# Start of an attention and expert kernel: constants awaited by user, contexts and zero rows by early DMAs, x's statistics in smaller parts

## The chip, the cores and the metric

The kernel runs on one core of a Trainium2 chip. The metric is the device time of one execution in microseconds, as the median of several runs. One profiled execution gives the trace that is read here.

## The reference

x is 32 batches of 100 rows of 256, ctx is 32 batches of 361 rows. All in fp32:

```python
def xattn(encoded, decoded, ...):             # 16 heads of 16
    q = decoded @ Wq.T + bq; k = encoded @ Wk.T + bk; v = encoded @ Wv.T + bv
    attn = softmax(einsum('bhqd,bhkd->bhqk', q, k)); z = einsum('bhqk,bhkd->bhqd', attn, v)
    y = z + decoded                           # heads joined
    return layernorm(y) * gamma + beta
def ffn(x, ...):                              # 8 experts, the best 2 for each row
    z = layernorm(x) * ln_g + ln_b
    w = top2(softmax(z @ rW + rb)), made to sum to 1
    return x + sum_e w_e * (gelu(z @ W1[e] + b1[e]) @ W2[e] + b2[e])
x = x + xattn(ctx, layernorm(x), ...)
x = x + ffn(layernorm(x), ...)
```

## The kernel before

The program has two parts. The first is attention and the router's logits, for one batch after another. The second sorts rows to experts and computes the experts. The change touches the first 80 us of the first part.

Each engine has its own instruction stream, written out by hand, and semaphores join them. `pipeline` calls `iteration(turn, i)` for i from -3 to 34. In iteration i the projections of K and Q are made for batch i+3 (called a), V's projection and the row maxima for batch i+1 (b), scores, exponentials and values for batch i (c), and the rest of the work for earlier ones. An iteration has twelve slots s. So iteration -3 makes K and Q of batch 0, iteration -2 those of batch 1, and iteration -1 has the first row maxima, those of batch 0.

K and Q are split into three bf16 parts each (k_part, q_part). DMAs copy the parts, per head, into 96 rows of k_stack and q_stack (slots 0 to 2 by batch), six DMAs for each (L262, L266). Rows 96 to 124 hold zeros. Rows 125 to 127 of k_stack hold ones, rows 125 to 127 of q_stack the three parts of the negated row maximum (m_part, L277). The row maxima use rows 0 to 124 (`score_rows`, L424), so the zero rows must be there; the scores use all 128 (L447).

GpSimd zeroes rows 96 to 127 of both stacks (L307, L309) after x's first variance. SyncE's queue starts all loads in the order written: the first eight batches of x, wk, the context of batch 0, ten more constants and so on, three further loads of x, then waits for both memsets, copies the ones rows, and only then enters its first iteration, which loads the context of batch 1 (L256). All 13 constants count on one semaphore (const_loaded), for all of which TensorE, ScalarE, VectorE and GpSimd wait before their first iteration. x's statistics run on VectorE in rounds of eight batches (`x_statistics`: bn_stats, L625, then eight small steps, L630 to L637), GpSimd raises the variance to -0.5 (L303), and VectorE forms the offset (L639). The first round stands ahead of everything, the other three at the end of iteration -3.

Of the kernel before, what the change touches and what calls it, by code (L numbers as in the profile page):

```python
# [27 lines left out]
TINY = 1e-30  # L28
SCORES_LAG, GUARD_LAG, VALUES_LAG = 4, 5, 7
# [57 lines left out]
def build(nc, x, ctx_t, wq_t, bq, wk_t, bk, wv_t, bv, gamma, beta, ln_g, ln_b, rw, rb, w1, b1, w2, b2,  # L87
          ident_d, route_c, sum_c, zscr, zf_d, odd_d, out):
    es = ExitStack()
    with es:  # L90
# [20 lines left out]
        const_loaded = sem("const_loaded")  # L111
        N_CONST = 13
        ones_loaded = sem("ones_loaded")
        stacks_zeroed = sem("stacks_zeroed")
        w1_loaded = sem("w1_loaded")
        x2_step = sem("x2_step")
        memsets, pad_written, ones_written = sem("memsets"), sem("pad_written"), sem("ones_written")
# [7 lines left out]
        with att:  # L125
# [14 lines left out]
            k_part = sb(att, "k_part", [128, 3, 3, 2, KEYS], BF16)  # L140
            ones_row = sb(att, "ones_row", [128 - MROW, KEYS], BF16)
# [75 lines left out]
            def _(sp):  # L217
                xv = x.rearrange("b q d -> q b d")

                def load_x(k):  # L220
                    sp.dma_start(x_all[:, 8 * k:8 * k + 8, :], xv[:, 8 * k:8 * k + 8, :]).then_inc(x_loaded[k], 16)
# [5 lines left out]
                sp.dma_start(ident[:], ident_d).then_inc(const_loaded, 16)  # L227
                sp.dma_start(wq_s[:], wq_t).then_inc(const_loaded, 16)
                sp.dma_start(wv_s[:], wv_t).then_inc(const_loaded, 16)
                sp.dma_start(bq_s[:], bq).then_inc(const_loaded, 16)  # L230
                sp.dma_start(bk_s[:], bk).then_inc(const_loaded, 16)
                sp.dma_start(bv_s[:], bv.unsqueeze(0).broadcast_to([128, D])).then_inc(const_loaded, 16)
                for dst, src in zip(row_c, (gamma, beta, ln_g, ln_b)):
                    sp.dma_start(dst[:], src.unsqueeze(0).broadcast_to([Q, D])).then_inc(const_loaded, 16)
                sp.dma_start(rw_s[:], rw.rearrange("(c p) e -> p c e", p=128)).then_inc(const_loaded, 16)
                sp.dma_start(rb_s[:], rb.unsqueeze(0).broadcast_to([Q, E])).then_inc(const_loaded, 16)
                for k in range(1, 4):
                    load_x(k)
                sp.wait_ge(pad_written, 2)
                sp.wait_ge(ones_written, 1)  # L240
                sp.wait_ge(stacks_zeroed, 2)
                sp.dma_start(k_stack[MROW:128].rearrange("r s h k -> r (s h) k"),
                             ones_row[:].unsqueeze(1).broadcast_to([128 - MROW, 3 * H, KEYS])).then_inc(ones_loaded, 16)

                def iteration(turn, i):
# [7 lines left out]
                    if n.valid():  # L253

                        after(sp, v_done, 2 * (n.index - 2))
                        sp.dma_start(ct[:, n.slot, :, 0:KEYS], ctx_t[n.index]).then_inc(ctx_loaded[n.slot], 16)  # L256
                    if w.valid():

                        sp.wait_ge(low_ready, 2 * w.index + 1)
                        after(sp, s_t_done, NG * w.index - NG * 2)  # L260
                        for g, s in enumerate(PROD):
                            sp.dma_start(k_stack[g:ROWS:len(PROD), w.slot].rearrange("r h k -> r (h k)"),  # L262
                                         k_part[:, w.slot, s].rearrange("p t k -> p (t k)")).then_inc(k_stacked[w.slot], 16)
                        sp.wait_ge(low_ready, 2 * w.index + 2)
                        for g, s in enumerate(QPART):
                            sp.dma_start(q_stack[g:ROWS:len(PROD), w.slot].rearrange("r h k -> r (h k)"),  # L266
                                         q_part[:, w.slot, s].rearrange("p t k -> p (t k)")).then_inc(q_stacked[w.slot], 16)
                    if d.valid():
# [23 lines left out]
            def _(pool):  # L292

                for n, (dst, fill) in enumerate(((half[:], -0.5), (v_aug[:, :, :, DH:32], 0.0), (v_aug[:, :, :, DH:DH + 1], 1.0))):
                    nc.gpsimd.memset(dst, fill).then_inc(memsets, 1)
                    pool.wait_ge(memsets, n + 1)
                g = nc.gpsimd

                def inverse_deviation_x(k):

                    pool.wait_ge(ln0_step, 8 * (k + 1))
                    part = slice(8 * k, 8 * k + 8)
                    g.tensor_tensor(rstd0[:, part], ln0[0][:, part], half[:].broadcast_to([Q, 8]), ALU.pow).then_inc(rstd0_ready, 1)  # L303

                inverse_deviation_x(0)
                pool.wait_ge(rstd0_ready, 1)
# [3 lines left out]
                pool.wait_ge(stacks_zeroed, 2)  # L310
                for k in range(4):
                    pool.wait_ge(x_loaded[k], 16)
                pool.wait_ge(const_loaded, 16 * N_CONST)

                def iteration(turn, i):
                    a, b, e = (Batch(turn, i + k) for k in (3, 1, -2))

# [44 lines left out]
                    for k in X_ROUNDS.get(i, ()) if a.known else ():  # L362
                        inverse_deviation_x(k)
# [4 lines left out]
            def _(pe):  # L368
                def project(b, item):
# [4 lines left out]
                    if item < 4:  # L374
                        t, c = item // 2, item % 2
                        if item == 0:
                            pe.wait_ge(ctx_loaded[b.slot], 16 * b.turn + 16)
# [11 lines left out]
                    elif item == 4:  # L389
                        pe.wait_ge(d_ready, b.index + 1)  # L390
# [13 lines left out]
                    else:  # L404
                        kt = item - 7
                        if kt == 0:
# [78 lines left out]
                def router(f):  # L485
                    pe.wait_ge(zft_copied, f.index + 1)
# [4 lines left out]
                pe.wait_ge(const_loaded, 16 * N_CONST)  # L491
# [30 lines left out]
            def _(act):  # L522
# [41 lines left out]

                act.wait_ge(const_loaded, 16 * N_CONST)
                act.wait_ge(nb0_ready, 1)

                def iteration(turn, i):
                    a, b, d, e, f = (Batch(turn, i + k) for k in (3, 1, -1, -2, -3))
                    if a.known and i == 2:  # L570
                        act.wait_ge(nb0_ready, 4)
                    for s in range(NG):
                        if a.valid() and s == X_SLOTS[0]:
                            normalised(a, drow, d_ready)
# [30 lines left out]
            def _(dve):  # L605
# [13 lines left out]
                def x_statistics(k):  # L619

                    dve.wait_ge(x_loaded[k], 16)
                    with dve.Fori(2 * k, 2 * k + 2) as t:
                        for j in range(4):
                            b = t * 4 + j if j else t * 4
                            v.bn_stats(stats0[:, b, :], x_all[:, b, :]).then_inc(stats0_done, 1)  # L625
                    dve.wait_ge(stats0_done, 8 * (k + 1))
                    part = slice(8 * k, 8 * k + 8)
# [9 lines left out]
                    step0(v.tensor_tensor(l0, l2, l1, ALU.add))  # L637
                    dve.wait_ge(rstd0_ready, k + 1)
                    v.scalar_tensor_tensor(nb0[:, part], mean0[:, part], -1.0, rstd0[:, part], ALU.mult, ALU.mult).then_inc(nb0_ready, 1)  # L639

                x_statistics(0)
                dve.wait_ge(const_loaded, 16 * N_CONST)

# [94 lines left out]
                def iteration(turn, i):  # L738
                    a, b, d, e, f = (Batch(turn, i + k) for k in (3, 1, -1, -2, -3))
                    for s in range(NG):  # L740
# [11 lines left out]
                        for h in heads_now[1:]:  # L752
                            row_max(b, h)
                        r = b if DVE_ITEMS.get(s, 0) >= 4 else a
# [21 lines left out]
                    for k in X_ROUNDS.get(i, ()) if a.known else ():  # L776
                        x_statistics(k)
# [387 lines left out]
X_ROUNDS = {-3: (1, 2, 3)}  # L1165
# [50 lines left out]
```

## Time and profile before

| | |
|---|---|
| median of 3 runs | 1077.88 us (1077.68 to 1085.16) |
| profiled execution | 1080.67 us, its span 1078.9 us |
| TensorE busy | 847.9 us (79%) |
| VectorE busy | 784.9 us (73%) |
| ScalarE busy | 481.0 us (45%) |
| GpSimd busy | 615.8 us (57%) |
| mean granted TensorE clock | 0.900 |

The span runs from the first to the last instruction. Busy time counts computing instructions. A DMA share of 1.00 means that all 16 DMA engines are at work.

### The profile page before, as it was taken

The page shows a single profiled execution, that of the slowest core. Times are in us where ns is not written, and L with a number is a line of the kernel's source. Part 1 is how long each engine was busy: PE and PEld are TensorE (multiplying, and loading weights), DVE is VectorE, ACT ScalarE, POOL GpSimd, SP SyncE. Part 2 cuts the span into 40 slices and gives each one's busy share as a digit, 9 for nine tenths or more (in the row PEclk, how much of TensorE's full clock was granted, in tenths as well). Part 3 has the DMA queues.
Part 4 walks back from the last instruction along what each step waited for, and adds up shares of the span by engine and source line. Part 5 has one row for each costly group of instructions (what it writes and reads, how often), then busy time and mean ns, then how long its engine had stood idle before and what let it go on. Part 6 is the DMA issues. An engine that isn't in the chain of part 4 may idle for free. (4 is left out here: it accounts for less than half of the span.)

```text
span 1078.9 us, 27269 instructions
## 1 busy us (share of the span) xinstructions
PE 847.9 (79%) x7982; PEld 594.6 (55%) x7983; DVE 784.9 (73%) x2424; ACT 481.0 (45%) x1188; POOL 615.8 (57%) x644
## 2 busy tenths in 40 slices
PE   2188988888888888888888888887103999999990
PEld 1055555555555545555555555454102999999980
DVE  3769889888998888889888988884286455555550
ACT  2025555555555555555555555544101444443430
POOL 5522455665565556655665566655416577777760
PEclk9589899999999999999999999975555999999995
DMA  6445455445544553455444544623390344344436
GB/s 187 87 100 112 85 131 122 87 99 120 123 87 96 129 115 86 101 129 111 88 98 121 120 88 101 150 52 71 99 306 24 50 64 70 64 65 66 66 54 125
DMA packets 157222, 109.25 MB, mean 101 GB/s; under 512 B 69439, under 2 KB 151079, under 8 KB 156615
## 3 DMA queue, kind: packets, MB, share of 16 engines
q1 hardware_dynamic: 145783, 91.04, 36.0%
q0 software_dynamic: 11360, 17.37, 9.7%
q8 instruction: 23, 0.38, 0.2%
q14 instruction: 56, 0.46, 0.1%
HBM read 40.20 MB, written 23.88 MB: 59 GB/s over the span
## 5 line engine op out<-in xcount | busy, mean ns | idle before, releaser
L676 DVE TENSOR_REDUCE negmax<-s_row 100x1 f32<-100x361 f32 x512 | 250.4, 520 | 22.8 <-PE s_row L424 22.5
L563 ACT ACTIVATE p_t<-s_t 128x400 f32<-128x400 f32 (+1 forms) x384 | 185.7, 497 | 129.2 <-PE s_t L447 128.6
L690 DVE TENSOR_SCALAR p_t<-p_t 128x400 f32<-128x400 f32 (+1 forms) x384 | 184.3, 482 | 39.4 <-ACT p_t L563 33.2
L424 PE MATMUL s_row<-k_stack,q_stack 125*128 125x361 bf16 x512 | 142.7, 329 | 53.0 <-DVE negmax L676 44.9
L321 POOL TENSOR_TENSOR rstd<-var,half 100x1 f32<-100x1 f32 x96 | 73.9, 770 | 162.2 <-DVE var L730 162.2
L459 PE MATMUL zt<-p_t,v_aug 128*32 128x100 f32 (+1 forms) x3072 | 152.8, 273 | 1.4 <-DVE p_t L690 1.0
L447 PE MATMUL s_t<-q_stack,k_stack 128*128 128x100 bf16 (+1 forms) x1536 | 146.6, 221 | 1.6 <-ACT p_t L563 1.0
L447 PEld LDWEIGHTS s_t<-q_stack,k_stack 128*128 128x128 bf16 (+1 forms) x1536 | 92.4, 112 | 60.0 <-issue 50.8
L385 PE MATMUL pj<-ct,wk_s 128*128 128x361 f32 x256 | 94.4, 494 | 37.7 <-DMA ct<-in_ctx_t 21.1
L904 PE MATMUL p_h<-zgt,w_k 128*128 128x128 f32 x912 | 113.3, 278 | 2.1 <-DVE w_k L1127 2.0
L904 PEld LDWEIGHTS p_h<-zgt,w_k 128*128 128x128 f32 x912 | 108.0, 194 | 3.1 <-DVE w_k L1127 2.4
L412 PE MATMUL pj<-wv_s,ct 128*128 128x256 f32 x384 | 107.8, 405 | 0.0
L913 PE MATMUL p_y<-w_s,hidt 128*128 x456 | 107.7, 379 | 0.0
L459 PEld LDWEIGHTS zt<-p_t,v_aug 128*32 128x32 f32 (+1 forms) x3072 | 62.5, 111 | 77.3 <-issue 49.7
L950 ACT ACTIVATE hidt<-p_h,b_k 128x128 f32<-128x128 f32 x228 | 65.2, 368 | 81.1 <-PE p_h L904 78.3
L424 PEld LDWEIGHTS s_row<-k_stack,q_stack 125*128 125x128 bf16 x512 | 44.8, 99 | 93.9 <-DVE negmax L676 88.6
L913 PEld LDWEIGHTS p_y<-w_s,hidt 128*128 128x128 f32 x456 | 82.4, 190 | 8.9
L385 PEld LDWEIGHTS pj<-ct,wk_s 128*128 128x128 f32 x256 | 47.3, 197 | 61.4 <-DMA ct<-in_ctx_t 21.3
L412 PEld LDWEIGHTS pj<-wv_s,ct 128*128 128x128 f32 x384 | 73.1, 204 | 8.9 <-issue 0.9
L344 POOL TENSOR_TENSOR v_aug<-v_pos,v_neg 128x768 f32<-128x768 f32 x32 | 58.4, 1825 | 33.0 <-DVE v_pos L670 33.0
L539 ACT ACTIVATE k_part<-pj,bk_s 128x361 bf16<-128x361 f32 x64 | 36.1, 564 | 91.0 <-PE pj L385 91.0
L983 POOL DMA_INDIRECT zg<-zf_d,idx_g x57 | 62.0, 1088 | 22.1 <-issue 17.1
(152 smaller groups left out, 1392.1 us busy)
## 6 DMA issues: line engine op xcount, KB each, us to landing
k_stack<-k_part SPq DMA_DIRECT2D x192, 180.5 KB, 4.2
q_stack<-q_part SPq DMA_DIRECT2D x192, 64.0 KB, 3.1
ct<-in_ctx_t SPq DMA_DIRECT2D x32, 361.0 KB, 3.9
w_s<-in_w SPq DMA_DIRECT2D x16, 512.0 KB, 5.4
x_all<-in_x SPq DMA_DIRECT2D x4, 800.0 KB
zscr<-zn SPq DMA_DIRECT2D x32, 100.0 KB
z_in<-zscr SPq DMA_DIRECT2D x32, 100.0 KB
zf_d<-zf_s SPq DMA_DIRECT2D x32, 100.0 KB
```

The source lines that it names most:

```text
L321: g.tensor_tensor(rstd[:], var[:], half[:], ALU.pow).then_inc(rstd_ready, 1)
L385: last = nc.tensor.matmul(pj[1 - t][:, 0:KEYS], wk_s[:, c, t * 128:t * 128 + 128], ct[:, b.slot, c, 0:KEYS], start=(c == 0), stop=(c == 1))
L412: last = nc.tensor.matmul(bank[:, kt % 2 * D:kt % 2 * D + D], ct[:, b.slot, c, kt * 128:kt * 128 + 128], wv_s[:, c, :], start=(c == 0), st ...
L424: nc.tensor.matmul(s_row[h % 2][:, 0:KEYS], q_stack[0:MROW, b.slot, h, :], k_stack[0:MROW, b.slot, h, 0:KEYS], start=True, stop=True).then ...
L447: last = nc.tensor.matmul(s_t[g % 2][0:n, j * Q:j * Q + Q], k_stack[:, b.slot, h, kt * 128:kt * 128 + n], q_stack[:, b.slot, h, 0:Q], star ...
L459: last = nc.tensor.matmul(zt[32 * j:32 * j + 32, grp * Q:grp * Q + Q], v_aug[0:n, b.slot, kt * H + 4 * grp + j, :], p_t[0:n, g % 4, j * Q: ...
L563: nc.scalar.activation(p_t[0:n, g % 4, :], s_t[g % 2][0:n, 0:4 * Q], ACT.Exp).then_inc(exp_done, 1)
L676: v.tensor_reduce(negmax[:, h:h + 1], s_row[h % 2][0:Q, 0:KEYS], AXIS.X, ALU.max, negate=True).then_inc(max_done, 1)
L690: v.tensor_scalar(p_t[0:n, g % 4, :], p_t[0:n, g % 4, :], 0.0, None, ALU.max).then_inc(p_ready, 1)
L904: last = nc.tensor.matmul(p_h[k.slot][:, j * 128:j * 128 + 128], w1_k[:, k.slot, c, j * 128:j * 128 + 128], zgt[:, k.slot, c * 128:c * 128 ...
L913: last = nc.tensor.matmul(p_y[k.slot][:, 0:D], hidt[:, k.slot, c * 128:c * 128 + 128], w2_s[:, c, bass.ds(e, 1), :].rearrange("p e f -> p ...
L950: nc.scalar.activation(hidt[:, k.slot, j * 128:j * 128 + 128], p_h[k.slot][:, j * 128:j * 128 + 128], ACT.Gelu, bias=b1_k[:, k.slot, j:j + ...
```

## The change

- Constants count on four semaphores by user (k_const, q_const, v_const, tail_const), and each user waits where it needs them first.
- SyncE's queue starts with wk, the contexts of batches 0 and 1, V's constants, zero rows, and the context of batch 2. Batch 3's context follows batch 1's stack loads.
- ScalarE's queue loads x's first 4 batches, ident, wq, bq, and x's next 8; the other 20 batches of x in two loads at the start of its iteration -1.
- GpSimd zeroes a strip of 29 rows (zero_rows), and three DMAs copy it, repeated along each row, into rows 96 to 124: slot 0 of k_stack and all of q_stack early, slots 1 and 2 of k_stack in iteration -1, ahead of the ones rows, the tail's constants and batch 1's stack loads.
- x's statistics come in parts of 4, 8 and 20 batches. The last 20 are spread over slots 0 to 9 of iterations 0 and 1.

```diff
+X_LOADS = [slice(0, FIRST), slice(FIRST, 12), slice(12, 22), slice(22, B)]
+X_PER = {-1: 0, 0: 10, 1: 10}
+X_PARTS = [slice(0, FIRST), slice(FIRST, 12), slice(12, B)]
...
+            zero_rows = sb(att, "zero_rows", [MROW - ROWS, 8 * QPAD], BF16)
...
             @blk.sync
             def _(sp):
-                load_x(0)
-                sp.dma_start(wk_s[:], wk_t).then_inc(const_loaded, 16)
+                sp.dma_start(wk_s[:], wk_t).then_inc(k_const, 16)
                 sp.wait_ge(pad_written, 1)
                 sp.dma_start(ct[:, 0, :, 0:KEYS], ctx_t[0]).then_inc(ctx_loaded[0], 16)
...
+                sp.dma_start(bk_s[:], bk).then_inc(k_const, 16)
+                sp.dma_start(ct[:, 1, :, 0:KEYS], ctx_t[1]).then_inc(ctx_loaded[1], 16)
+                sp.dma_start(wv_s[:], wv_t).then_inc(v_const, 16)
+                sp.dma_start(bv_s[:], bv.unsqueeze(0).broadcast_to([128, D])).then_inc(v_const, 16)
+                sp.wait_ge(zeros_written, 1)
+
+                def zero_keys(slots, done):
+                    stack = k_stack[ROWS:MROW, slots].rearrange("r s h k -> r (s h k)").rearrange("r (a n) -> r a n", n=2 * KEYS)
+                    sp.dma_start(stack, zero_rows[:, 0:2 * KEYS].unsqueeze(1).broadcast_to([MROW - ROWS, stack.shape[1], 2 * KEYS])).then_inc(done, 16)
+
+                zero_keys(slice(0, 1), stacks_zeroed)
+                sp.dma_start(q_stack[ROWS:MROW].rearrange("r s h k -> r (s h k)").rearrange("r (a n) -> r a n", n=8 * QPAD),
+                             zero_rows[:, 0:8 * QPAD].unsqueeze(1).broadcast_to([MROW - ROWS, 3 * H // 8, 8 * QPAD])).then_inc(stacks_zeroed, 16)
+                sp.dma_start(ct[:, 2, :, 0:KEYS], ctx_t[2]).then_inc(ctx_loaded[2], 16)
                 sp.wait_ge(pad_written, 2)
-                sp.wait_ge(ones_written, 1)
-                sp.wait_ge(stacks_zeroed, 2)
-                sp.dma_start(k_stack[MROW:128].rearrange("r s h k -> r (s h) k"),
-                             ones_row[:].unsqueeze(1).broadcast_to([128 - MROW, 3 * H, KEYS])).then_inc(ones_loaded, 16)
+
+                def later_loads():
+                    zero_keys(slice(1, 3), others_zeroed)
+                    sp.wait_ge(ones_written, 1)
+                    sp.dma_start(k_stack[MROW:128].rearrange("r s h k -> r (s h) k"),
+                                 ones_row[:].unsqueeze(1).broadcast_to([128 - MROW, 3 * H, KEYS])).then_inc(ones_loaded, 16)
+                    for dst, src in zip(row_c, (gamma, beta, ln_g, ln_b)):
+                        sp.dma_start(dst[:], src.unsqueeze(0).broadcast_to([Q, D])).then_inc(tail_const, 16)
...
+                    if n.known and i == -1:
+                        later_loads()
...
             def _(pool):
+                nc.gpsimd.memset(zero_rows[:], 0.0).then_inc(zeros_written, 1)
...
-                g.memset(q_stack[ROWS:128], 0.0).then_inc(stacks_zeroed, 1)
-                pool.wait_ge(stacks_zeroed, 1)
-                g.memset(k_stack[ROWS:128], 0.0).then_inc(stacks_zeroed, 1)
...
             # TensorE, score_rows
                     if h == 0 and b.known and b.index == 0:
-                        pe.wait_ge(stacks_zeroed, 2)
+                        pe.wait_ge(stacks_zeroed, 32)
+                    if h == 0 and b.known and b.index == 1:
+                        pe.wait_ge(others_zeroed, 16)
...
             # ScalarE
-                act.wait_ge(const_loaded, 16 * N_CONST)
-                act.wait_ge(nb0_ready, 1)
+                act.dma_start(x_all[:, X_LOADS[0], :], xv[:, X_LOADS[0], :]).then_inc(x_loaded[0], 16)
+                act.dma_start(ident[:], ident_d).then_inc(q_const, 16)
+                act.dma_start(wq_s[:], wq_t).then_inc(q_const, 16)
+                act.dma_start(bq_s[:], bq).then_inc(q_const, 16)
+                act.dma_start(x_all[:, X_LOADS[1], :], xv[:, X_LOADS[1], :]).then_inc(x_loaded[1], 16)
+                act.wait_ge(k_const, 32)
...
+                    if a.known and i in (1, 2):
+                        act.wait_ge(nb0_ready, i + 1)
...
             # VectorE, iteration
+                        if a.known and i == -3 and s == 5:
+                            x_offset(0)
+                        if a.known and i in (-1, 0, 1) and s < X_PER[i]:
+                            b0 = 12 + sum(X_PER[j] for j in range(-1, i)) + s
...
+                            x_sums(range(b0, b0 + 1))
...
+                        if a.known and i == -3 and s == 4:
+                            x_variance(0)
...
+                    if a.known and i == 1:
+                        x_variance(2)
+                        x_offset(2)
```

On SyncE's queue the start of the program reads so before (a DMA's destination, its source, the destination's partitions first):

```order
L221 DMA x_all<-in_x 100x8x256
L224 DMA wk_s<-in_wk_t 128x512
L226 DMA ct<-in_ctx_t 128x2x361
...
L236 DMA rb_s<-in_rb 100x8
L221 DMA x_all<-in_x 100x8x256 x3
L242 DMA k_stack<-ones_row 3x48x361
L256 DMA ct<-in_ctx_t 128x2x361 x2
L262 DMA k_stack<-k_part 16x8x722 x6
L266 DMA q_stack<-q_part 16x8x256 x6
L256 DMA ct<-in_ctx_t 128x2x361
```

and so in the changed program, up to batch 1's stack loads:

```order
L228 DMA wv_s<-in_wv_t 128x512
L229 DMA bv_s<-in_bv 128x256
L234 DMA k_stack<-zero_rows 29x8x722
L237 DMA q_stack<-zero_rows 29x6x1024
L239 DMA ct<-in_ctx_t 128x2x361
L275 DMA k_stack<-k_part 16x8x722 x6
L279 DMA q_stack<-q_part 16x8x256 x6
L234 DMA k_stack<-zero_rows 29x16x722
L245 DMA k_stack<-ones_row 3x48x361
...
L275 DMA k_stack<-k_part 16x8x722 x6
L279 DMA q_stack<-q_part 16x8x256 x6
L266 DMA ct<-in_ctx_t 128x2x361
```

Three transfers of 29 partitions now stand on this queue, two ahead of batch 0's stack loads and one ahead of batch 1's, and x's loads are gone from it.

On VectorE in iteration -3, the first K and Q, before:

```order
L639 SCALAR_TENSOR_TENSOR nb<-mean,rstd 100x8
L655 SCALAR_TENSOR_TENSOR k_rest<-pj,bk_s,k_part 128x361 x2
L649 SCALAR_TENSOR_TENSOR q_rest<-pj,bq_s,q_part 128x100 x2
```

and in the changed program:

```order
L653 BN_STATS stats<-x_all 100x6 x4
L688 SCALAR_TENSOR_TENSOR k_rest<-pj,bk_s,k_part 128x361
L660 TENSOR_TENSOR ln_0<-stats 100x4
...
L667 TENSOR_TENSOR ln_0<-ln_2,ln_1 100x4
L672 SCALAR_TENSOR_TENSOR nb<-mean,rstd 100x4
L688 SCALAR_TENSOR_TENSOR k_rest<-pj,bk_s,k_part 128x361
L682 SCALAR_TENSOR_TENSOR q_rest<-pj,bq_s,q_part 128x100 x2
L653 BN_STATS stats<-x_all 100x6 x8
```

The variance steps and the offset moved from ahead of the first half of K to between its two halves.

## Rows read from the trace of the kernel before

**Rows 1.** The page, busy time of each engine.
```profile
PE 847.9 (79%) x7982; PEld 594.6 (55%) x7983; DVE 784.9 (73%) x2424; ACT 481.0 (45%) x1188; POOL 615.8 (57%) x644
```

**Rows 2.** Busy time by stretches, all engines; then clock, DMA share, GB/s.
```profile
10.00:20.00 10.00, 4.08 (x7) 2.42 (x8) 3.98 (x16) 2.45 (x3) 6.29 (x2) 1.00 0.68 199
20.00:30.00 10.00, 2.45 (x12) 1.54 (x10) 5.63 (x14) 3.03 (x7) 9.94 (x2) 0.66 0.37 120
30.00:40.00 10.00, 0.00 (x0) 0.00 (x0) 7.89 (x8) 0.00 (x0) 8.86 (x4) 0.50 0.16 37
60.00:70.00 10.00, 8.28 (x35) 4.77 (x33) 8.67 (x19) 2.16 (x4) 0.22 (x2) 0.96 0.64 152
80.00:90.00 10.00, 8.73 (x105) 5.39 (x102) 9.59 (x23) 6.07 (x16) 3.98 (x3) 1.00 0.62 131
90.00:100.00 10.00, 9.79 (x95) 5.57 (x92) 8.44 (x20) 4.88 (x10) 0.00 (x0) 1.00 0.53 119
```

**Rows 3.** TensorE's waits in the first 60 us: total, times, longest.
```profile
PE pj L385 <- DMA ct<-in_ctx_t: 21.1, 1, 21.1
PE pj L385 <- DMA rb_s<-in_rb: 15.9, 1, 15.9
```

**Rows 4.** Timeline of SyncE's queue: start, length.
```profile
35.29 0.93 SPq L242 DMA_DIRECT2D k_stack<-ones_row  x1
36.26 3.78 SPq L256 DMA_DIRECT2D ct<-in_ctx_t  x2
40.09 4.26 SPq L262 DMA_DIRECT2D k_stack<-k_part  x6
44.39 3.81 SPq L266 DMA_DIRECT2D q_stack<-q_part  x6
```

**Rows 5.** Timeline of GpSimd.
```profile
13.65 1.68 POOL L303 TENSOR_TENSOR rstd<-ln,half 100x8 f32<-100x8 f32 x1 [10.33 <-DVE ln L637]
15.39 5.21 POOL L307 MEMSET q_stack<- 32x6144 bf16 x1
20.66 14.53 POOL L309 MEMSET k_stack<- 32x17328 bf16 x1
```

**Rows 6.** Context loads issued at 36 to 37 us; all DMA traffic from 35 to 40.
```profile
L256 SPq DMA_DIRECT2D ct<-in_ctx_t x2: 613/1869/3125, 36.3 to 36.9; - x2
...
DMA to landing us min/median/max: 9.0/9.6/10.2
...
DMA packets 317, 0.37 MB, mean 74 GB/s; under 512 B 12, under 2 KB 317, under 8 KB 317
```

**Rows 7.** Timeline of TensorE.
```profile
15.91 4.58 PE L385 MATMUL pj<-ct,wk_s 128*128 128x361 f32 x8 [15.91 <-DMA rb_s<-in_rb]
...
45.32 5.18 PE L385 MATMUL pj<-ct,wk_s 128*128 128x361 f32 x8 [21.06 <-DMA ct<-in_ctx_t]
...
59.32 0.81 PE L424 MATMUL s_row<-k_stack,q_stack 125*128 125x361 bf16 x2
...
71.75 1.96 PE L412 MATMUL pj<-wv_s,ct 128*128 128x256 f32 x4
73.50 0.81 PE L424 MATMUL s_row<-k_stack,q_stack 125*128 125x361 bf16 x2
```

**Rows 8.** Stretches; last three columns TensorE clock, DMA share, GB/s.
```profile
5.00:7.00 2.00, 1.00 1.11 231
12.00:14.00 2.00, 1.00 0.65 156
20.00:24.00 4.00, 0.90 0.68 223
37.00:37.50 0.50, 0.50 0.15 22
38.00:38.50 0.50, 0.00 (x0) 0.00 (x0) 0.00 (x0) 0.00 (x0) 0.49 (x1) 0.50 0.95 286
39.00:40.50 1.50, 0.50 0.24 27
67.00:70.00 3.00, 1.00 1.10 232
```

**Rows 9.** Timeline of VectorE.
```profile
9.14 2.71 DVE L625 BATCH_NORM_STATS2 stats<-x_all  x8 [7.47 <-DMA x_all<-in_x]
11.89 0.17 DVE L630 TENSOR_TENSOR ln<-stats 100x8 f32<-100x8 f32 x1
...
13.33 0.17 DVE L637 TENSOR_TENSOR ln<-ln,ln 100x8 f32<-100x8 f32 x1
...
15.45 0.17 DVE L639 SCALAR_TENSOR_TENSOR nb<-mean,rstd 100x8 f32<-100x8 f32 x1 [1.96 <-POOL rstd L303]
```

More of the change, by code:

```diff
@@ L301, in inverse_deviation_x @@
                     pool.wait_ge(ln0_step, 8 * (k + 1))
-                    part = slice(8 * k, 8 * k + 8)
-                    g.tensor_tensor(rstd0[:, part], ln0[0][:, part], half[:].broadcast_to([Q, 8]), ALU.pow).then_inc(rstd0_ready, 1)
+                    g.tensor_tensor(rstd0[:, X_PARTS[k]], ln0[0][:, X_PARTS[k]], half[:].broadcast_to([Q, X_PARTS[k].stop - X_PARTS[k].start]), ALU.pow).then_inc(rstd0_ready, 1)
                 inverse_deviation_x(0)
-                pool.wait_ge(rstd0_ready, 1)
-                g.memset(q_stack[ROWS:128], 0.0).then_inc(stacks_zeroed, 1)
-                pool.wait_ge(stacks_zeroed, 1)
-                g.memset(k_stack[ROWS:128], 0.0).then_inc(stacks_zeroed, 1)
[L310 to L313, printed above, removed]
                 def iteration(turn, i):
                     a, b, e = (Batch(turn, i + k) for k in (3, 1, -2))
+                    if a.known and i == 2:
+                        for k in range(4):
+                            pool.wait_ge(x_loaded[k], 16)
+                        pool.wait_ge(tail_const, 16 * 6)
                     def inverse_deviation(k):
@@ L361, in iteration @@
                         g.tensor_tensor(q_part[:, a.slot, 2, :, 0:Q], q_rest[:], q_part[:, a.slot, 1, :, 0:Q], ALU.subtract).then_inc(low_ready, 1)
-                    for k in X_ROUNDS.get(i, ()) if a.known else ():
-                        inverse_deviation_x(k)
+                    if a.known and i in (-3, 1):
+                        inverse_deviation_x({-3: 1, 1: 2}[i])
                 pipeline(pool, iteration, first=2)
@@ L376, in project @@
                         if item == 0:
+                            if b.known and b.index == 0:
+                                pe.wait_ge(k_const, 32)
                             pe.wait_ge(ctx_loaded[b.slot], 16 * b.turn + 16)
@@ L389, in project @@
                     elif item == 4:
+                        if b.known and b.index == 0:
+                            pe.wait_ge(q_const, 48)
                         pe.wait_ge(d_ready, b.index + 1)
@@ L405, in project @@
                         kt = item - 7
+                        if b.known and b.index == 0:
+                            pe.wait_ge(v_const, 32)
                         if kt == 0:
@@ L485, in router @@
                 def router(f):
+                    if f.known and f.index == 0:
+                        pe.wait_ge(tail_const, 16 * 6)
                     pe.wait_ge(zft_copied, f.index + 1)
@@ L617, in step0, with x_sums, x_variance @@
                     dve.wait_ge(ln0_step, count[0])
[L619 to L627, printed above, removed]
+                def x_sums(batches):
+                    for b in batches:
+                        v.bn_stats(stats0[:, b, :], x_all[:, b, :]).then_inc(stats0_done, 1)
+                def x_variance(k):
+                    part = X_PARTS[k]
+                    dve.wait_ge(stats0_done, part.stop)
                     me, mo = stats0[:, part, 1], stats0[:, part, 4]
@@ L637, in x_statistics, with x_offset @@
                     step0(v.tensor_tensor(l0, l2, l1, ALU.add))
+                def x_offset(k):
+                    part = X_PARTS[k]
                     dve.wait_ge(rstd0_ready, k + 1)
                     v.scalar_tensor_tensor(nb0[:, part], mean0[:, part], -1.0, rstd0[:, part], ALU.mult, ALU.mult).then_inc(nb0_ready, 1)
[L641 to L642 removed]
+                dve.wait_ge(x_loaded[0], 16)
+                x_sums(range(B)[X_LOADS[0]])
                 def projections(a, item):
@@ L775, in iteration @@
                             max_low(b)
-                    for k in X_ROUNDS.get(i, ()) if a.known else ():
-                        x_statistics(k)
+                    if a.known and i == -3:
+                        dve.wait_ge(x_loaded[1], 16)
+                        x_sums(range(B)[X_LOADS[1]])
+                        x_variance(1)
+                    if a.known and i == -2:
+                        x_offset(1)
+                    if a.known and i == 1:
+                        x_variance(2)
+                        x_offset(2)
                 pipeline(dve, iteration)
```

47 lines of the change are left out of this document (23 added, 24 removed).

## Prediction

> **What bounds the kernel now.** I read the busy times first [rows 1]: TensorE 79%, VectorE 73%. In the attention part both run near their limit once work is flowing, so the batches follow each other at a fixed pace, and what happens in the first 75 us moves the whole program. So I read the start by stretches [rows 2]: TensorE does 4.08 us of work in 10 to 20 us, 2.45 in the next ten, none in 30 to 40, and is filled only from 60. Its waits say why [rows 3]: 15.9 us for the last constant (rb_s), 21.1 us for batch 1's context. The DMA list of SyncE's queue and of GpSimd [rows 4, 5] show the second wait's origin: the two context loads stand behind the wait for the zeroed stacks, and GpSimd's memset of k_stack ends at 35.2. The row of the two contexts shows one more thing: the first lands 9.0 us after its issue at 36.3, so at 45.3, just when TensorE resumes [rows 6, 7]. Two marks are what I carry: the first row-maximum product of batch 0 runs at 59.3 (call it R0), that of batch 1 at 73.5 (R1) [rows 7]. Work after R1 keeps its pace, so the change is worth the shift of R1, plus what it adds behind it.
>
> **What is gained in compute.** Without the wait for all constants K of batch 0 needs wk, bk and ct, 0.63 MB on SyncE's queue, with as much of ScalarE's 1.6 MB moved beside it: 1.26 MB at the 231 GB/s of the first loads [rows 8] is 5.5 us, from about 3 us on, and a microsecond for the last pieces: about 9.5 instead of 15.9. The chain of batch 0 becomes about 2.8 us longer, since variance, the power (1.68 us) and the offset now stand between the two halves of k_rest (order of VectorE, front part; [rows 5]). K of batch 1 can follow at once, at about 21 instead of 45.3; eight more statistics (2.71 us) and their variance (1.65 us, eight steps 0.2 apart) [rows 9] delay it little. TensorE and the stack loads of batch 0 (8.1 us of issue, [rows 4]) would then be through at 32 or 33: R0 26 to 27 us earlier. If that were all, this would be the result.
>
> **What the zero rows cost.** The two GpSimd memsets (5.21 and 14.53 us) become three DMAs of 29 partitions: k slot 0, 335 KB; q_stack, 356 KB (29 x 12288 B); k slots 1 and 2, 670 KB. The price hangs on how many of the 16 DMA engines a transfer of 29 partitions uses. The trace answers for other shapes [rows 8]. x's later loads, 100 partitions, hold a share of 0.65 to 0.68 of 16 engines, 10 to 11 of them. The ones rows, 3 partitions, hold 0.15 while they are alone, 2.4 of 16, so 3 with gaps. The stack loads, 16 partitions into which 128 are copied, hold all (1.10). So 16 partitions use more engines than 100: the count does not follow the size. What fits all three is the largest number up to 16 that divides the partition counts on both sides: 10, 3, 16. For 29, a prime, it is 1.
>
> The Trainium skill ("DMA: Bandwidth & Descriptors", section "Why a DMA increments its semaphore by 16 and not by 1") states this rule, with 100 partitions on 10 engines and 127 on 1, always the lowest-numbered ones; the shares above agree with it for 10 and 3. By the general advice in the skill's overview that DMAs of all queues interleave on the same 16 engines, without this rule, the zero rows would be 1.36 MB on 16 engines, about 6 us of transfer, and the change a gain (second rival below).
>
> So I take it that every zero byte passes one engine, and that a later transfer on that queue has its share of that engine behind it. That second step is seen in the trace too: the first context (0.37 MB) was issued right after the ones rows and landed 9.0 us later, although the stretch at 38 us moved 286 GB/s. From 35 to 40 us 0.37 MB moved in all [rows 6, 8], as much as 13/16 of that context and most of the ones rows; 39 to 40.5 shows 27 GB/s, the three engines of the ones rows alone. So 13 engines were done and waiting, and the context landed with the last three.
>
> **Pace of one engine.** Stack loads, the same 1444-byte pieces within SBUF: 232 GB/s over 16, 14.5 GB/s each. x's loads: 223 GB/s over 10, 22 GB/s. Ones rows alone: 22 to 27 GB/s over 3, 7 to 9 [rows 8]. I take 14.5 for the zeros, as it is the same kind and size of piece, and keep 22 and 8.7 as ends.
>
> **The sum on that engine until R1.** Transfers of 128 partitions leave 1/16 of their bytes on it, those of 100 partitions 1/10. Before the first zeros or beside them: wk 16, ct 0 and 1 46, wv 16, bv 8, ident 4, wq 16, first x loads 41 and 82: 229 KB, with all engines at 14.4 GB/s [rows 8] 16 us, from 3 us on. Zeros of k slot 0 and q, 691 KB: 48 us. ct 2 and the twelve stack loads of batch 0 (1.5 MB / 16): 117 KB, 5 us at 22. R0 is then about 72 us, 12 later than now, although TensorE stood ready at 32. Behind that: zeros of slots 1 and 2, 670 KB, 46 us; ones rows 35 KB, four constant rows 41 KB, the two last x loads from ScalarE's queue 205 KB, stack loads of batch 1 94 KB: 375 KB, 17 us at 22. R1 is about 135 instead of 73.5: **61 us later**. Ends: with all 2.08 MB at 22 GB/s R1 = 3 + 95 = 98, 24 later; with the zeros at 8.7 (156 us) and the rest as above R1 = 197, 124 later.
>
> The two x loads are taken at 22, their own rate, though they share the engine; the SyncE-queued row constants are wanted only by the tail of batch 0 and by the router, two iterations on, and cost nothing there.
>
> **Behind R1.** Twenty statistics go into VectorE's busy slots of iterations 0 and 1. Eight took 2.71 us [rows 9], so 6.8 us in all; VectorE is 80 to 95% busy there [rows 2], TensorE as well, so half may be hidden: +3.4, bounds 0 and 6.8. The variance of the last 20 (1.65) and the offset's wait for GpSimd (1.96, [rows 9]) stand at the end of iteration 1, and ScalarE waits for the offset ahead of iteration 2's first exponential, with VectorE's guards behind that: +3, bounds 0 and 3.8. The clock: TensorE idles for some 60 us, and idle time left it at 0.50 in this trace too, 0.96 again from 60 to 70 us [rows 2]; the eight products of the second K took 5.18 us against 4.58 of the first [rows 7], +2, bounds 0 and 5. Batch 1's V (its first half, 1.96 us [rows 7]) is done during the wait: -2. Sum: 61 + 3.4 + 3 + 2 - 2 = **+67 to +69 us**. Taken against the profiled execution, 1080.67 with span 1078.9; that lies 2.8 above the median of 1077.88, and the shift is applied to the median, so **1146 us**.
>
> Where I chose: the engine count and 14.5 GB/s. Everything else in the sum is under 5 us. What hides the gains of the first part is plain: TensorE's early start is worth nothing while zeroed rows gate the row maxima of batch 0 (stacks_zeroed) and batch 1 (others_zeroed plus the stack loads behind it).
>
> **Rivals.**
> First, one engine, but faster, as x's loads go (22 GB/s): R1 24 later, +5 behind, so about 1107. For it: nothing else uses most of the fabric while the zeros run. Against: these are copies within SBUF, and both kinds of those in the trace are slower per engine.
> Second, **faster than before**: the three zero transfers spread over 10 to 16 engines. Then DMA work is 4.0 MB up to 21 us, R0 is 33. In iteration -1 the queues carry zeros 0.67, constants 0.5, x 2.05 and stacks 1.5 MB, 4.7 MB at 215 GB/s, 22 us from 30, so batch 1's stacks land at 52 instead of the 47 that 14.3 us of row maxima would allow; with +6 to +7 behind R1 this is -21 + 6, about 1063 (range 1052 to 1072). For it: x's loads of 100 partitions get 10. Against: 3 partitions get 3, and no reading that gives 29 many engines explains 100 getting fewer than 16 do. It decides from about four engines: then all zeros need 1.36 MB / 58 GB/s = 23 us, and start and end are about even.
> Third, the pace of the ones rows (8.7): R1 124 later, about 1205 to 1215. For it: source and target lie in the same partition, as there. Against: their pieces are half as long, so a fixed time for each piece would explain their rate.
> That the change is not what it says in another respect, that all zeros finish early and row maxima start near 33, is the second rival's picture.
>
> **How the numbers follow.** One engine at 11 to 19 GB/s 0.56 (1120 to 1178), one engine faster 0.2 (1098 to 1120), one engine slower 0.1 (1178 to 1220), spread 0.12 (1052 to 1072), something near zero 0.02. A range of 1098 to 1200 leaves out the spread case, the near-zero one and half of the slow one, nearly 2 in 10. Faster by over 1% 0.11, within 1% (what a measurement of this kernel can tell from nothing) 0.03, slower 0.86.
>
> **What the profile after would show.** Right: K of batch 0 near 9.5 us; a long stretch with a DMA share of about 0.06 (1 of 16) and some 10 to 22 GB/s; the first row maxima waiting for k_stack or q_stack near 70; TensorE idle again before batch 1's row maxima, R1 near 135; SyncE not waiting, since the wait is in the transfer. From R1 on the distance between batches as before. Wrong: a share over 0.5 during the zeros and R0 near 33 (second rival). The prediction fails most if the engine count is not 1; if it is 1, the time of the three transfers scales it.

## The result, and the profile after

The changed kernel takes 1140.03 us in the median of 4 runs (1136.44 to 1143.49), the kernel before 1079.78 (1077.68 to 1085.16, 4 runs): a ratio of 1.055, interval 1.049 to 1.061, 60 us slower. The profiled execution took 1142.34 us, its span 1140.4.

The page's busy line and the two queues of the profile after:

```profile
PE 862.8 (76%) x7982; PEld 602.9 (53%) x7983; DVE 776.4 (68%) x2415; ACT 481.5 (42%) x1188; POOL 594.9 (52%) x642
...
q1 hardware_dynamic: 142984, 88.80, 33.7%
...
q10 hardware_dynamic: 3672, 3.61, 1.3%
```

The engines do about the same work in a longer span [rows 1]; the second queue (q10) carries ScalarE's loads. Where the time went is seen at the start. TensorE's waits in the first 120 us, after, answering to [rows 3]:

```profile
PE s_row L443 <- DMA q_stack<-q_part: 55.5, 2, 32.8
PE pj L398 <- DMA bk_s<-in_bk: 9.2, 1, 9.2
```

The first K starts at 9.15 us instead of 15.9 and the second at 21.0 instead of 45.3, as the new waits allow. Then TensorE waits 55.5 us for the stack loads, in two waits of 32.8 and 22.7. Its timeline at R0 and R1 (the first row-maximum products of batches 0 and 1), answering to [rows 7]:

```profile
65.52 0.79 PE L443 MATMUL s_row<-k_stack,q_stack 125*128 125x361 bf16 x2 [32.79 <-DMA q_stack<-q_part]
...
79.55 1.96 PE L429 MATMUL pj<-wv_s,ct 128*128 128x256 f32 x4
104.25 0.78 PE L443 MATMUL s_row<-k_stack,q_stack 125*128 125x361 bf16 x2 [22.73 <-DMA q_stack<-q_part]
```

R0 is 65.5 (59.3 before), R1 104.25 (73.5 before). What the DMA engines did in that time, by stretches (last three columns: TensorE clock, DMA share, GB/s), answering to [rows 8]:

```profile
5.00:9.00 4.00, 0.00 (x0) 0.00 (x0) 1.41 (x4) 0.00 (x0) 0.00 (x0) 1.00 1.07 302
16.00:20.00 4.00, 1.38 (x6) 1.11 (x7) 0.67 (x2) 1.63 (x3) 1.15 (x2) 0.57 0.07 24
24.00:30.00 6.00, 2.44 (x10) 1.53 (x9) 3.50 (x14) 1.81 (x4) 1.99 (x2) 0.74 0.07 24
65.00:70.00 5.00, 4.48 (x12) 3.21 (x13) 2.54 (x5) 0.00 (x0) 0.00 (x0) 0.50 0.07 24
80.00:85.00 5.00, 1.51 (x4) 0.67 (x2) 1.39 (x5) 1.49 (x5) 1.22 (x2) 0.84 0.07 24
```

A share of 0.07 is one engine of 16 (0.0625), and it moves 24 GB/s. While x's last loads and batch 0's stack loads run, from about 33 to 60 us, the share is higher; from 60 to 85 it is one engine again. SyncE's queue (start, length of the issue), answering to [rows 4]:

```profile
4.74 0.86 SPq L234 DMA_DIRECT2D k_stack<-zero_rows  x1
5.65 16.58 SPq L237 DMA_DIRECT2D q_stack<-zero_rows  x1
22.27 14.76 SPq L239 DMA_DIRECT2D ct<-in_ctx_t  x1
37.14 12.44 SPq L275 DMA_DIRECT2D k_stack<-k_part  x6
49.62 7.54 SPq L279 DMA_DIRECT2D q_stack<-q_part  x6
57.20 0.78 SPq L234 DMA_DIRECT2D k_stack<-zero_rows  x1
58.03 27.98 SPq L245 DMA_DIRECT2D k_stack<-ones_row  x1
```

Before, a context was issued in 0.6 to 3.1 us [rows 6] and the ones rows in 0.93 [rows 4]; now the issues behind a transfer of zeros take 16.6, 14.8 and 28.0 us. Two of these lengths are those of the zeros ahead of them: q_stack's 356 KB need 14.8 us at 24 GB/s, slots 1 and 2 with 670 KB need 27.9. So SyncE is held in the next issue until about the time when the zeros ahead of it are through. No view shows what holds it. Batch 0's stack loads, wanted from 21 on, were not even issued before 37, and batch 1's only at 92.93.

The rest of the 61 us is found with one mark for each batch, the store of zn (L272, L287). Marks of batches 0, 1 and 31, the last, in the trace before:

```profile
107.34 0.32 SPq L272 DMA_DIRECT2D zscr<-zn  x1
129.61 0.29 SPq L272 DMA_DIRECT2D zscr<-zn  x1
...
758.70 0.29 SPq L272 DMA_DIRECT2D zscr<-zn  x1
```

The same marks after:

```profile
141.94 0.33 SPq L287 DMA_DIRECT2D zscr<-zn  x1
169.76 0.30 SPq L287 DMA_DIRECT2D zscr<-zn  x1
...
817.70 0.30 SPq L287 DMA_DIRECT2D zscr<-zn  x1
```

The shift is 30.8 us at R1, 34.6 at the first mark, 40.2 at the second, 59.0 at the last, and 61.5 at the end. Up to the second mark this is the forecast's kind of loss. The 18.8 us between the second mark and the last are not: there both kernels run the same loop. Its waits differ mainly in one place. VectorE's idle times at the loop's restart, one turn (three iterations, so three batches) apart, in the trace after:

```profile
242.33 0.65 DVE L723 TENSOR_SCALAR p_t<-p_t 128x400 f32<-128x400 f32 x2 [3.89 <-ACT p_t L583]
307.88 0.65 DVE L723 TENSOR_SCALAR p_t<-p_t 128x400 f32<-128x400 f32 x2 [3.99 <-ACT p_t L583]
```

and before:

```profile
262.19 0.65 DVE L690 TENSOR_SCALAR p_t<-p_t 128x400 f32<-128x400 f32 x2 [2.97 <-ACT p_t L563]
326.56 0.64 DVE L690 TENSOR_SCALAR p_t<-p_t 128x400 f32<-128x400 f32 x2 [2.72 <-ACT p_t L563]
```

The named releaser isn't it: after, ScalarE's last exponentials in question began at 305.04, took 0.88 together and were through 2 us before VectorE went on at 307.88.

### The profile page after: what moved, and what is told of

Same layout as the page of the kernel before. It is cut to its first block and busy times, and to the rows that moved or that the text cites. A ratio compares the mean times of both kernels' runs of the same rounds, so it can differ in the third digit from the quotient of the medians.

```text
span 1140.4 us, 27176 instructions
## 1 busy us (share of the span) xinstructions
PE 862.8 (76%) x7982; PEld 602.9 (53%) x7983; DVE 776.4 (68%) x2415; ACT 481.5 (42%) x1188; POOL 594.9 (52%) x642
## 5 line engine op out<-in xcount | busy, mean ns | idle before, releaser
L443 PE MATMUL s_row<-k_stack,q_stack 125*128 125x361 bf16 x512 | 145.3, 335 | 120.2 <-DVE negmax L709 57.3
L466 PE MATMUL s_t<-q_stack,k_stack 128*128 128x100 bf16 (+1 forms) x1536 | 149.0, 223 | 4.2 <-ACT p_t L583 4.2
L443 PEld LDWEIGHTS s_row<-k_stack,q_stack 125*128 125x128 bf16 x512 | 45.3, 100 | 162.2 <-DVE negmax L709 98.7
L429 PE MATMUL pj<-wv_s,ct 128*128 128x256 f32 x384 | 111.3, 415 | 0.0
L398 PEld LDWEIGHTS pj<-ct,wk_s 128*128 128x128 f32 x256 | 49.3, 205 | 34.5 <-issue 14.7
```

What stands on the lines that cost most here:

```text
L398: last = nc.tensor.matmul(pj[1 - t][:, 0:KEYS], wk_s[:, c, t * 128:t * 128 + 128], ct[:, b.slot, c, 0:KEYS], start=(c == 0), stop=(c == 1))
L429: last = nc.tensor.matmul(bank[:, kt % 2 * D:kt % 2 * D + D], ct[:, b.slot, c, kt * 128:kt * 128 + 128], wv_s[:, c, :], start=(c == 0), st ...
L466: last = nc.tensor.matmul(s_t[g % 2][0:n, j * Q:j * Q + Q], k_stack[:, b.slot, h, kt * 128:kt * 128 + n], q_stack[:, b.slot, h, 0:Q], star ...
```

## The experiments

Three questions: is it one DMA engine; what did the rest of the change cost or bring; and why does the loop, which nobody edited, run slower.

**1. Zeros spread over more engines.** In the changed kernel, each zero transfer in three row groups:

```diff
+                ZPARTS = ((0, 16), (16, 12), (28, 1))
...
-                    stack = k_stack[ROWS:MROW, slots]...
-                    sp.dma_start(stack, zero_rows[:, 0:2 * KEYS]...broadcast_to([MROW - ROWS, ...])).then_inc(done, 16)
+                    for r0, nr in ZPARTS:
+                        stack = k_stack[ROWS + r0:ROWS + r0 + nr, slots]...
+                        sp.dma_start(stack, zero_rows[r0:r0 + nr, 0:2 * KEYS]...broadcast_to([nr, ...])).then_inc(done, 16)
```

> The changed kernel, with each of the three zero transfers cut into row groups of 16, 12 and 1, which the common-divisor reading puts on 16, 12 and 6 to 16 DMA engines; bytes and order of the queue stay. If the one engine is the cause: the stretches with a DMA share of 0.07 vanish, batch 0's first row maximum comes at 33 to 36 us instead of 65.5, batch 1's at 50 to 55 instead of 105, and the time falls by at least 50 us, to 1065 to 1090. If the cause is the other parts (scattered statistics, two queues competing): the time stays over 1120. If the queue itself is slow with such copies within SBUF whatever the engines: 1100 to 1130.

Measured: 1098.72 us (1096.36 to 1101.53), 41 us less than the changed kernel; 1.0147 of before (1.0118 to 1.0175). The share stays at 0.74 to 1.15 from 9 to 24 us (in the changed kernel it falls to 0.07 at 16), and R0 is 34.5, as one engine's absence would have it. The same bytes in the same order on the same queue: the engine count was the cause of R0's delay. The time missed its forecast of 1065 to 1090, though, and R1 its mark of 50 to 55. Two rows of TensorE's timeline:

```profile
34.51 0.81 PE L447 MATMUL s_row<-k_stack,q_stack 125*128 125x361 bf16 x2
...
63.27 0.78 PE L447 MATMUL s_row<-k_stack,q_stack 125*128 125x361 bf16 x2 [14.56 <-DMA q_stack<-q_part]
```

14.6 us of waiting for batch 1's stacks are left, in a stretch (40 to 60) with a DMA share of 0.79 to 0.92: contention, the mechanism of the second rival, and larger than the 5 us it had there. The loop is slow here too: 646.2 us from the second mark to the last, against 629.1 before.

**2. Zeros by GpSimd.** No zero bytes on a queue; memsets of q_stack and slot 0 first, slots 1 and 2 behind the third parts of batches 0 and 1:

```diff
-                nc.gpsimd.memset(zero_rows[:], 0.0).then_inc(zeros_written, 1)
+                nc.gpsimd.memset(q_stack[ROWS:MROW], 0.0).then_inc(stacks_zeroed, 1)
+                pool.wait_ge(stacks_zeroed, 1)
+                nc.gpsimd.memset(k_stack[ROWS:MROW, 0], 0.0).then_inc(stacks_zeroed, 1)
...
+                    if a.known and i in (-3, -2):
+                        pool.wait_ge(low_ready, 2 * a.index + 2)
+                        g.memset(k_stack[ROWS:MROW, i + 4], 0.0).then_inc(others_zeroed, 1)
```

> The changed kernel with its zero rows written by GpSimd again, in four memsets placed so that q_stack and slot 0 of k_stack come first and slots 1 and 2 after the third parts of batches 0 and 1; all other parts of the change stay. One-engine theory: no zero bytes on any queue, first row maxima at 33 and 48 to 50, time 1060 to 1075, faster than before by the earlier start (26 us) less 10 to 15 for the contention of the start and the statistics in iterations 0 and 1. If the distance between batches in the loop is larger because of the statistics part of the change, it stays 22.4 us a batch instead of 21.6 and the time is 1075 to 1085.

Measured: 1099.18 us (1097.57 to 1102.57), 1.0153 of before. That is 24 us over the first forecast and 14 over the second. R0 is 40.0 (TensorE's first product waited until 13.6 for GpSimd's small memset of v_aug behind the large ones, a fault of this kernel's order), R1 63.7 after 9.6 us of waiting for q_stack. The first mark is 5.9 us ahead of before's, the second 0.6, and the last, 778.2, is 19.5 behind. So the gain of the start is lost in iterations -1 to 1, and the loop's slowness is here too (649.2 us from the second mark to the last), without the one engine.

**3. Zero rows alone.** The kernel before, with only its memsets replaced:

```diff
-                g.memset(q_stack[ROWS:128], 0.0).then_inc(stacks_zeroed, 1)
...
-                g.memset(k_stack[ROWS:128], 0.0).then_inc(stacks_zeroed, 1)
...
+                for stack, n in ((k_stack, 2 * KEYS), (q_stack, 8 * QPAD)):
+                    dst = stack[ROWS:MROW]...
+                    sp.dma_start(dst, zero_rows[:, 0:n]...broadcast_to([MROW - ROWS, dst.shape[1], n])).then_inc(stacks_zeroed, 16)
```

> The kernel before, with its two memsets replaced by the zero strip and two transfers of 29 partitions ahead of the ones rows (1.36 MB at one engine's 24 GB/s is 57 us, behind x's loads that end at 26). One-engine theory: batch 1's context and the stack loads land behind them, first row maxima at 95 to 100 instead of 59, time 1110 to 1125. If the zero rows alone are harmless and the loss comes from their place in the new order: within 10 us of before. Distance between batches in the loop: 21.6 as before if the statistics part makes it longer, 22.4 if the late start or the larger memory map does.

Measured: 1124.45 us (1123.87 to 1126.26), 1.039 of before, as expected. Its stretches (the last two columns are share and GB/s) and TensorE's wait:

```profile
40.00:60.00 20.00, 0.00 (x0) 0.00 (x0) 4.42 (x18) 0.00 (x0) 2.31 (x2) 1.00 0.07 24
```

```profile
PE pj L386 <- DMA ct<-in_ctx_t: 64.0, 1, 64.0
```

One part of the change reproduces the one engine, its 24 GB/s and a loss of 43 us. It also repeats the blocked issues: behind k_stack's zeros (1.0 MB, 41.9 us at 24 GB/s) SyncE's issue of q_stack's zeros takes 40.82 us. And the loop is not slow here: the distances from the third mark to the 27th sum to 518.9 us, against 515.6 before and 534.4 in the changed kernel. This kernel has the larger memory map, but the old statistics code.

**4. The last offset later.** The kernel of 2, with x_offset(2) in slot 4 of iteration 2, and ScalarE's wait at that iteration's end:

```diff
                     if a.known and i == 1:
                         x_variance(2)
-                        x_offset(2)
...
+                        if a.known and i == 2 and s == 4:
+                            x_offset(2)
```

> As the kernel with four memsets, and the offset of the last 20 batches moved into slot 4 of iteration 2, with ScalarE waiting for it only at that iteration's end. In the changed kernel ScalarE waited 5.9 us for this offset and the batch there took 28 us instead of 22. If that wait is on the path: 4 to 6 us less than the kernel with four memsets. If it only takes up slack of that iteration: within 2 us of it.

Measured: 1092.87 us (1088.49 to 1096.87), 6.3 less than in 2. In 2 ScalarE's waits from 90 to 132 us were led by

```profile
ACT drow L567 <- DVE nb L669: 5.9, 1, 5.9
```

and that row is gone; the second mark moved from 129.05 to 123.10. The wait was wholly on the path. It costs 5.9, not 3, in the main because GpSimd's power takes 3.54 us for 20 columns (1.05 for 4, 1.65 for 8).

**5. The loop at its old place in the program.** What still differs between kernels with a slow and a fast loop is the code ahead of it. In the built program 305 of VectorE's instructions stood ahead of its loop of 317 before, and 261 after, since the statistics loops became straight code. 44 memsets of one element in VectorE's idle start move it back:

```diff
+                for n in range(44):
+                    v.memset(zero_rows[0:1, n:n + 1], 0.0)
                 count = [0]
```

> The four-memset kernel with the late offset, plus 44 one-element memsets on VectorE ahead of the first statistics, where it is idle. They bring VectorE's loop from instruction 261 to 305 of its program, where it stood before the change; nothing else moves. In every kernel with the changed statistics VectorE stands idle 3.9 to 4.1 us at each restart of its loop, in those with the old statistics 2.7 to 3.1, and every third batch is some 2.5 us longer. If the place of the loop in the program makes this: the stall is back at 2.75, and the time is 10 to 20 us less than the kernel without the memsets. If it comes from something else in the change (other engines' programs, semaphores, the clock): same time within 4 us.

Measured: 1077.71 us (1075.69 to 1079.19), 15.2 less than in 4, with 44 instructions more. One turn's restart:

```profile
254.19 0.65 DVE L724 TENSOR_SCALAR p_t<-p_t 128x400 f32<-128x400 f32 x2 [2.75 <-ACT p_t L580]
```

**6. The kernel before, moved.** The same with 20 memsets (of a tile of its own) in the kernel before: loop at 325.

> The kernel before, plus 20 one-element memsets on VectorE behind its three first ones. They bring its loop from instruction 305 to 325, the same place modulo 64 as in the changed kernel (261). If the place modulo 64 or a divisor of it makes the longer stall: 3.9 us at each restart instead of 2.75 and 10 to 20 us slower than before. If only the old and the new code differ in something else: no difference over 3 us.

Measured: 1078.34 us (1072.88 to 1081.37), 0.9967 of before (0.9947 to 0.9988). The first reading falls: 325 is not slow but, if anything, better. No idle time over 1.2 us is left at the restart. So the remainder modulo 64, which 325 shares with 261, does not decide.

**7. x's loads early.** The kernel of 4, with x's last two loads at the start, and GpSimd's small memsets ahead of the large ones (the second edit is not shown):

```diff
-                act.dma_start(x_all[:, X_LOADS[1], :], ...)
+                for k in (1, 2, 3):
+                    act.dma_start(x_all[:, X_LOADS[k], :], ...)
...
-                    if a.known and i == -1:
-                        for k in (2, 3): act.dma_start(x_all[:, X_LOADS[k], :], ...)
```

> The four-memset kernel with the late offset, with the last two loads of x issued at the start on ScalarE's queue instead of in iteration -1, and GpSimd's small memsets ahead of the large ones. In the four-memset kernel TensorE waits 9.6 us for batch 1's q_stack at 54 us, while x's last 2 MB are under way. If that contention is the cause: this wait falls to under 2 us and the time by 7 to 11 us. If the stack loads are late for another reason (constants of the tail ahead of them, issue time of 8 us): within 3 us.

Measured: 1080.36 us (1074.55 to 1082.1), 12.5 less than in 4. R0 is 34.4 (the order of memsets, 5.7) and R1 comes without a wait on a stack load:

```profile
48.62 0.81 PE L441 MATMUL s_row<-k_stack,q_stack 125*128 125x361 bf16 x2
```

25 us ahead of before, the full gain of the early start. Two edits are in this run. The order of the memsets moved R0; that the wait at R1 went with x's last 2 MB is read from the loads: in 2 batch 1's q_stack loads were all issued by 49.9 us and TensorE waited for them until 63.7, here they were issued by 46.7 and had landed by 48.6. The times of 7 and of 4 lie 12.5 us apart, more than the 7 to 11 forecast, and the memsets' share of that was not measured by itself.

**8. Both.**

> The kernel with early loads of x plus the 44 one-element memsets. If both causes hold and add up, it is faster than before: 1060 to 1070, first row maxima at 33, batch 1's at 48 to 50. If the loop's stall isn't cured by the place of the loop: the same as without the 44 memsets, 1080 to 1090.

Measured: 1063.62 us (1061.85 to 1065.26), 0.9841 of before (0.9823 to 0.986), 16.7 less than in 7: the two add up. R0 and R1 are 36.2 and 50.1, 1.8 and 1.5 us behind 7; the memsets stand ahead of the first statistics.

**9. The changed kernel itself, with its loop moved back.** 44 memsets, to an idle tile:

```diff
+                for n in range(44):
+                    v.memset(t1[0:1, n:n + 1], 0.0)
```

> The changed kernel itself, one-engine zeros and all, plus 44 one-element memsets on VectorE at the start, so that its loop stands at instruction 305 again. If the loop's place is a cause by itself, beside the zero rows: 14 to 18 us less than the changed kernel, 1122 to 1127, stall at the loop's restart 2.7 to 3.1 us, batch marks 1 and 2 as in the changed kernel (near 170 and 192). If it mattered only with the short start: within 4 us of 1140.

Measured: 1120.68 us (1120.08 to 1122.24), 19.4 less than the changed kernel and a little more than forecast. Its second mark is 167.8 (169.8 there), its last 797.8 (817.7): from one to the other 630 us, against 629 before and 648 in the changed kernel. So 18.0 of the loop's 18.8 us are the place of the loop. The end of the program is 2.4 us shorter as well (300.3 us from the load of sums to the end, 300.4 before, 302.7 after), but from the last mark to the end the twelve traces range over 319.2 to 323.9 us whatever the place, so that part is not told from their spread.

**10. Loop at 325.** The kernel of 7 with 64 memsets.

> The kernel with early loads of x and 64 memsets, which put the loop at instruction 325. In the kernel before with its loop at 325 no idle time over 2.2 us was left at the restart. If the place alone sets the stall: no such idle time here either, and 2 to 5 us less than with 44 memsets, 1058 to 1062. If the stall depends on more than that engine's place: 1062 to 1066.

Measured: 1058.0 us (1055.32 to 1061.43), 0.9816 of before (0.9792 to 0.9839), 5.6 less than with 44, a little more than expected, and the fastest version, 21 us under the kernel before. As in 6, no idle time over 1.2 us is left at the restart, and every third batch takes 21.5 us instead of 22.2.

```profile
q14 instruction: 2, 0.02, 2.1%
...
q14 instruction: 1, 0.01, 0.9%
```

and in the whole execution, in the same order and then with the loop at 325 (10):

```profile
q14 instruction: 55, 0.45, 0.2%
...
q14 instruction: 56, 0.46, 0.1%
...
q14 instruction: 21, 0.17, 0.1%
```

At 261 all seven restarts have two such packets in the idle time, about 0.9 and 1.4 us after it began; at 305 (9) all seven have one. A whole turn has five in both. At 325, in 6 as in 10, the queue moves none from 260 to 620 us. VectorE's idle time comes and goes with the instructions that are loaded again at the restart.

## Why the prediction was right, and where it was not

**The sign and the mechanism held; the total held by luck, through two errors that nearly cancel** (30 us too many up to R1, mostly from the engine's pace, and 21 too few for the loop and the end). 1146 was forecast, 1140 measured. By the forecast's own steps:

- **Engine count: right.** From 3 partitions on 3 engines, 100 on 10 and 16 on 16 it read one engine for 29; the share is 0.07, and splitting the rows alone gives back 41 us (1). The Trainium skill's rule ("DMA: Bandwidth & Descriptors", section "Why a DMA increments its semaphore by 16 and not by 1") agrees with the share of 0.07 in the changed kernel and in 3.
- **Order on that engine: right, and worse.** Stack loads queue behind the zeros. "SyncE not waiting, since the wait is in the transfer" was wrong: its issues take up to 28 us, so the later transfers also start late on the 15 idle engines. With the zeros at 24 GB/s and the rest as it stands, the forecast's own sum gives R0 53 and R1 98; 65.5 and 104.25 were measured. The blocked issues are the likely reason for these 12 and 6 us, but no run separates them.
- **Pace of the engine: the mis-sized term.** 14.5 GB/s was taken from stack loads with all 16 engines at work; alone, one engine moves the same pieces at 24 (after, and in 3). All 1.36 MB of zeros need 57 us, not 94. R1 came 30.8 us late, not 61; the end "all at 22 GB/s" gave 24. The row to take was that of x's loads (22 GB/s for an engine, with six engines idle), not that of the most similar pieces with all 16 at work. The Trainium skill ("DMA: Bandwidth & Descriptors", section "Specifications") gives about 27 GiB/s for an engine, 29 GB/s; the measured 24 lies a sixth below it.
- **Gain in compute: right, and hidden as said.** First K forecast 9.5 and seen at 9.15, second 21 and 21.0. With the zeros out of the way it is worth 25 us at R1 (7).
- **Statistics in busy slots: right in size.** R1 to first mark grew by 3.9 us against 3.4 forecast. The terms for the clock (+2) and for batch 1's V (-2) are in the same stretch and were not separated.
- **Offset: too small.** 5.6 us between the marks, against 3 with a bound of 3.8. The power's time was taken from 8 columns for a call with 20.
- **Missing: the loop's place.** 18.8 us in the loop, and 2.5 at the end of the program, in no term and no rival. "From R1 on the distance between batches as before" was the wrong sentence. 9 shows that the number of VectorE's instructions ahead of the loop makes 18.0 of the 18.8; the 2.5 at the end are within the spread of the traces. Added up: R1 30.8, iteration 0 3.8, offset 5.6, loop 18.8, end 2.5: the 61.5 us of the two spans.

**The rivals.** The spread rival forecast 1063 where spreading gives 1099 (1): its contention was 15 us and not 5, it had 3 for the offset instead of 5.9, and nothing for the loop. With these three removed, and the zeros written by GpSimd, 1064 and 1058 are reached (8, 10). The first rival, one engine at 22 GB/s, was nearest in the mechanism; its 1107 is 33 us under the time, 21 of them the loop and the end.

**What stays open.** A restart costs 3.8 to 4.2 us with the loop at 261, mostly 2.7 to 3.1 at 305 and under 1.2 at 325, and the instruction queue's packets go with it (two, one, none). That VectorE waits for these packets is argued from their times, since no view names the engine they are for; and which places need them is not known from three places. Also open in part is how 1.1 us more per turn becomes 2.3 per turn. Two turns of the loop in the trace after (third column from the end: TensorE's granted clock):

```profile
307.90:378.10 70.20, 61.65 (x603) 38.64 (x603) 56.20 (x171) 36.36 (x84) 37.60 (x48) 0.88 0.45 99
...
511.90:577.30 65.40, 54.75 (x603) 34.30 (x603) 56.04 (x172) 35.90 (x84) 38.78 (x48) 1.00 0.49 106
```

Of six such turns the two at a clock of 1.00 take 65.4 and 65.6 us, the four at 0.88 to 0.97 take 66.2 to 70.2; before, turns at 1.00 take 64.4. So at full clock a turn is longer by 1.0 us, the size of the extra idle time, and the rest comes in turns of a lower clock. What lowers the clock there was not tested, and it is not the clock alone: before, turns at 0.97 take 64.5 to 65.5 us.

## What to carry to other kernels

Look at the partition count of every DMA ahead of the critical loads: 29 partitions ran on one engine, and what is queued behind waits for it. To price such a transfer, take a row of the trace in which other engines are idle too (x's loads, 22 GB/s an engine), not one with similar pieces and all 16 engines at work (14.5). And after any edit ahead of a long loop, compare the loop's own period, the idle time at its restart and the packets of the instruction queue: unedited code changed by 2.3 us a turn here through its place alone, and 44 instructions of no use got it back.

## What the runs showed of the hardware that was not expected

- One DMA engine alone, copying 1444 and 2048-byte pieces within SBUF, moves 24 GB/s; with all 16 busy an engine moved 14.5 in stack loads of 1444-byte and shorter pieces [rows 8].
- The issue of a DMA behind a one-engine transfer holds up SyncE for about that transfer's time: 28.0 us for the ones rows behind 670 KB (0.93 before [rows 4]), 14.8 behind 356 KB, 40.8 behind 1.0 MB in 3.
- VectorE idles at each restart of a 317-instruction loop for 3.8 to 4.2, mostly 2.7 to 3.1, or under 1.2 us by how many instructions stand ahead of it (261, 305, 325). In eight turns that made 19.4 us between 261 and 305 (9) and 22.4 between 261 and 325 (7, 10). The queue q14 loads two, one or no packets of instructions in that time.
- GpSimd's power took 1.05, 1.65 and 3.54 us for 4, 8 and 20 columns of 100 rows.
